# A post-norm decoder layer on one core: one visit per unit for attention's weighted values, two turns of duties, and six low parts on GpSimd

## What is computed

```python
x = layernorm(x + attention(x, w_qkv, w_o))        # 32 heads of 32, 8 key/value heads, RoPE, causal
x = layernorm(x + cross(x, ctx, Wq, bq, Wk, bk))   # softmax((xWq'+bq)(cWk'+bk)'/32) c
x = layernorm(x + ffn(x))                          # x @ W' + bias, W looked up from 4-bit codes
```

## Time and profile before

| | |
|---|---|
| runs, median (lowest to highest) | 1291.42 us (1290.22 to 1291.81) |
| the profiled execution, its own time | 1288.92 us |
| its span, first to last instruction | 1287.1 us |
| TensorE matmuls busy | 1263.6 us, 98% |
| VectorE busy | 901.6 us, 70% |
| ScalarE busy | 531.4 us, 41% |
| GpSimd busy | 477.2 us, 37% |
| granted TensorE clock, mean | 0.999 of full |

### The profile page before, as it was taken

One profiled execution on the slowest core, in us unless ns is written; L12 is line 12 of the kernel. 1 busy time (PEld: TensorE's weight loads), 2 busy tenths in 40 slices (PEclk: granted clock), 3 DMA queues, 4 the chain that ended last, 5 costly groups with the idle time before them and its releaser, 6 DMA issues.

```text
span 1287.1 us, 25356 instructions
## 1 busy us (share of the span) xinstructions
PE 1263.6 (98%) x8230; PEld 1041.7 (81%) x8230; DVE 901.6 (70%) x2526; ACT 531.4 (41%) x1597; POOL 477.2 (37%) x413
## 2 busy tenths in 40 slices
PE   8999999998999999999999999999999999999997
PEld 6887888997777777777777887888888888888886
DVE  7999898578888888888876974353443636556665
ACT  4131212457777777777760223243433433100110
POOL 3512122345656656656550000544334450222221
PEclk9999999999999999999999999999999999999999
DMA  7165435463864344344343215125251419212221
GB/s 280 68 213 170 144 132 203 141 208 113 236 182 120 118 134 127 114 135 134 121 127 106 68 34 173 41 82 181 66 196 64 149 49 358 100 65 98 98 87 60
DMA packets 135450, 170.43 MB, mean 132 GB/s; under 512 B 36688, under 2 KB 100176, under 8 KB 134736
## 3 DMA queue, kind: packets, MB, share of 16 engines
q1 hardware_dynamic: 135376, 169.47, 40.6%
HBM read 112.80 MB, written 56.62 MB: 132 GB/s over the span
## 4 chain that ended last, share of the span: by engine, by line
PE 72%; issue 12%; DVE 8%; POOL 4%; SPq 2%; DMA 1%; ACT 1%; POOLq 0%; DVEq 0%; ACTq 0%
PE bank L863 13%; PE bank L677 11%; PE bank L679 11%; PE bank L678 11%; PE bank L805 7%; PE bank L763 4%; PE bank L790 4%; POOL x2b L1984 3%; PE bank L834 3%; PE bank L838 2%; PE bank L726 1%; DVE bits L1482 1%; PE bank L982 1%; DVE pick_b L1521 1%; DVE pick_c L1510 1%
## 5 line engine op out<-in xcount | busy, mean ns | idle before, releaser
L1907 POOL TENSOR_TENSOR prob<-prob,rinv 128x512 f32<-128x512 f32 x192 | 205.5, 1071 | 204.8 <-DVE rinv L1570 204.7
L1187 ACT ACTIVATE prob<-bank,nmax 128x256 f32<-128x256 f32 (+1 forms) x512 | 211.3, 427 | 90.6 <-DVE nmax L1562 83.9
L1562 DVE CUSTOM_DVE_ANT_0 bank<-bank,mask 128x256 f32<-128x256 f32 (+1 forms) x512 | 169.3, 383 | 7.3 <-PE bank L790 3.7
L805 PE MATMUL bank<-ident,prob 128*128 128x128 f32 x768 | 122.0, 282 | 2.8 <-ACT probT L1117 2.8
L805 PEld LDWEIGHTS bank<-ident,prob 128*128 128x128 f32 x768 | 85.4, 141 | 35.9 <-issue 16.7
L1187 ACT ACTIVATION_READ_ACCUMULATOR prob<-bank,nmax 128x1 f32 x512 | 108.1, 211 | 0.0
L1723 DVE SCALAR_TENSOR_TENSOR k_lo<-bank,bA,k_hi 128x512 fp32r<-128x512 f32 x32 | 24.0, 751 | 115.1 <-ACT k_hi L1320 114.5
L790 PE MATMUL bank<-k,q 96*128 96x256 f32 (+1 forms) x512 | 102.8, 303 | 1.7 <-DMA vv<-v_scr 1.7
L863 PE MATMUL bank<-wo_hi,att_hi 128*128 128x512 f32 x256 | 103.9, 406 | 0.0
L677 PE MATMUL bank<-f_hi,x2T_hi 128*128 128x512 f32 x256 | 101.0, 395 | 0.8 <-DVE x2T_lo L1418 0.8
L677 PE MATMUL bank<-cT_hi,m_hi 128*128 128x512 f32 x256 | 100.4, 392 | 0.7 <-DVE cT_lo L1418 0.7
(11 more groups left out here) (201 smaller groups left out, 3145.9 us busy)
## 6 DMA issues: line engine op xcount, KB each, us to landing
q<-qk_scr SPq DMA_DIRECT2D x192, 128.0 KB, 2.4
x_st<-x_scr SPq DMA_DIRECT2D x32, 512.0 KB, 3.8
qk_scr<-rot SPq DMA_DIRECT2D x60, 256.0 KB, 2.6
xc_in<-x_cols SPq DMA_DIRECT2D x32, 256.0 KB, 4.7
y<-x SPq DMA_DIRECT2D x16, 512.0 KB, 3.6
x_scr<-y SPq DMA_DIRECT2D x16, 512.0 KB, 2.7
cx_in<-ctx_in SPq DMA_DIRECT2D x16, 512.0 KB, 4.9
x_scr<-x_st SPq DMA_DIRECT2D x16, 512.0 KB, 3.3
```

What stands on the lines that cost most here:

```text
L805: mm = nc.tensor.transpose(tb[:, at * P:(at + 1) * P], prob[:, k % 4, c:c + P], ident[:, :])
L1187: mm = nc.scalar.activation(prob[:, k % 4, i * keys:(i + 1) * keys], SBANK[pos][:, i * keys:(i + 1) * keys], ACT.Exp, bias=nmax[:, k % 4, ...
L1562: mm = nc.vector.tensor_tensor_reduce(part, part, mask[:, 2 * P - keys:2 * P], 1.0, BIGGEST, ALU.add, ALU.min, nmax[:, k % 4, i:i + 1])
L1907: nc.gpsimd.tensor_tensor(pr, pr, rinv[:, k % 4, 0:n].unsqueeze(2).to_broadcast([P, n, keys]), ALU.mult)\
```

## The change

Four edits.

1. `weighted` does nothing at positions 0 and 1. At position 2 it waits for all three copies of the transposes and does both halves: two groups of four, `pv_done`, one group of four, `pv_done`.
2. A turn of a decoded block is made inside the pair that follows, behind its second slice (`TURN_KT`, 12 matmuls in), instead of ahead of it.
3. VectorE's order where x's low parts and decoding steps alternate is given by a table (`X_LOW_AFTER`): in group 0 all eight low parts first; in groups 1 and 2 two decoding steps stand ahead of the first low part.
4. The six low parts of w_o that are made in the first batch go from VectorE to GpSimd, with a semaphore of their own for the other two; block 5's step moves from 22 to 21, the last two blocks' and the last RoPE item's steps of batch 1 move by one.

```diff
+        X_LOW_AFTER = ((0,) * KT, (2, 2, 3, 3, 4, 4, 5, 5), (2, 2, 3, 3, 4, 5, 5, 6))
+        TURN_KT = 2
-        WO_STEPS = {(0, 12): 2, (0, 14): 3, (0, 18): 0, (0, 19): 1, (0, 20): 4, (0, 22): 5, (1, 4): 6, (1, 6): 7}
+        WO_STEPS = {(0, 12): 2, (0, 14): 3, (0, 18): 0, (0, 19): 1, (0, 20): 4, (0, 21): 5, (1, 5): 6, (1, 7): 7}
...
                 for kt in range(KT):
+                    if turned is not None and kt == TURN_KT:
+                        turn_f(turned)
...
-                pos, unit = k % 3, k // 3
-                if pos == 0:
+                unit = k // 3
+                if k % 3 < 2:
                     return
-                taken(b, k - 1)
-                taken(b, k)
+                for i in range(3):
+                    taken(b, k - 2 + i)
...
-                if pos == 1:
-                    wait(pe, att_ready, KVH * b + unit)
-                    for t in range(2):
-                        for h in range(REP):
-                            src = probT[:, (k - 1 + h // 2) % 4, (2 * t + h % 2) * P:(2 * t + h % 2 + 1) * P]
...
-                else:
+                wait(pe, att_ready, KVH * b + unit)
+                for t in range(2):
                     for h in range(REP):
-                        mm = nc.tensor.matmul(OBANK[HD * h:HD * (h + 1), 0:P], v[:, 0, :],
-                                              probT[:, k % 4, h * P:(h + 1) * P], start=True, stop=True,
-                                              skip_group_check=True)
+                        src = probT[:, (k - 2 + h // 2) % 4, (2 * t + h % 2) * P:(2 * t + h % 2 + 1) * P]
+                        mm = nc.tensor.matmul(OBANK[HD * h:HD * (h + 1), P:2 * P], v[:, t, :], src,
+                                              start=t == 0, stop=t == 1, skip_group_check=True)
+                mm.then_inc(pv_done, 1)
+                for h in range(REP):
+                    mm = nc.tensor.matmul(OBANK[HD * h:HD * (h + 1), 0:P], v[:, 0, :],
+                                          probT[:, k % 4, h * P:(h + 1) * P], start=True, stop=True,
+                                          skip_group_check=True)
                 mm.then_inc(pv_done, 1)
...
-                    if age == 1 and k == 2:
+                    if age == 1 and k == 3:
                         rope_item(11)
...
-                    if age < 2 and (age, k - 1) in WO_STEPS:
+                    if age == 1 and (age, k - 1) in WO_STEPS:
                         kt = WO_STEPS[age, k - 1]
                         dve.wait_ge(wo_hi_ready, WO_TURN[kt] + 1)
-                        low(wo_lo[:, kt, :], wo_in[:, kt, :], wo_hi[:, kt, :]).then_inc(wo_lo_ready, 1)
+                        low(wo_lo[:, kt, :], wo_in[:, kt, :], wo_hi[:, kt, :]).then_inc(wo_lo2_ready, 1)
...
+                    if age == 0 and (0, k - 1) in WO_STEPS:
+                        kt = WO_STEPS[0, k - 1]
+                        pool.wait_ge(wo_hi_ready, WO_TURN[kt] + 1)
+                        nc.gpsimd.tensor_tensor(wo_lo[:, kt, :], wo_in[:, kt, :], wo_hi[:, kt, :].bitcast(F32), ALU.subtract)\
+                            .then_inc(wo_lo_ready, 1)
```

More of the change, by code:

```diff
@@ L243, in decoder_layer @@
         fps_ready, f_hi_ready, f_lo_ready, f_stored = sem("fps_ready"), sem("f_hi_ready"), sem("f_lo_ready"), sem("f_stored")
-        wo_ld, wo_hi_ready, wo_lo_ready = sems("wo_ld", KT // 2), sem("wo_hi_ready"), sem("wo_lo_ready")
+        wo_ld, wo_hi_ready, wo_lo_ready, wo_lo2_ready = (
+            sems("wo_ld", KT // 2), sem("wo_hi_ready"), sem("wo_lo_ready"), sem("wo_lo2_ready"))
         wq_first_ld, wq_ld, wq_hi_ready, wq_lo_ready = sem("wq_first_ld"), sem("wq_ld"), sem("wq_hi_ready"), sem("wq_lo_ready")
@@ L330, in decoder_layer @@
         LOW_STEP = {23: (0, 0), 0: (1, 1), 2: (1, 2), 6: (1, 3)}
-        WO_STEPS = {(0, 12): 2, (0, 14): 3, (0, 18): 0, (0, 19): 1, (0, 20): 4, (0, 22): 5, (1, 4): 6, (1, 6): 7}
+        WO_STEPS = {(0, 12): 2, (0, 14): 3, (0, 18): 0, (0, 19): 1, (0, 20): 4, (0, 21): 5, (1, 5): 6, (1, 7): 7}
+        WO_EARLY = sum(age == 0 for age, _ in WO_STEPS)
         WO_TURN = {kt: i for i, kt in enumerate(WO_STEPS.values())}
@@ L694, in turn_f, with qk_pair @@
                 turn(decode_tiles(b)[1][:, :].bitcast(F32), banks, fps_ready)
-            def qk_pair(g, c):
+            def qk_pair(g, c, turned=None):
                 n = PAIRS * g + c
@@ L730, in values @@
                         mm.then_inc(x_lo_used if low else x_used, 1)
-            for at in ORDER:
+            for i, at in enumerate(ORDER):
                 if at[1] < PAIRS:
-                    qk_pair(*at)
+                    qk_pair(*at, F_TURN.get(ORDER[i - 1]) if i else None)
                 else:
@@ L738, in _ @@
                     pe.wait_ge(consts_step, 4)
-                if at in F_TURN:
-                    turn_f(F_TURN[at])
             def fill(k):
@@ L818, in weighted @@
             def weighted(b, k):
-                pos, unit = k % 3, k // 3
-                if pos == 0:
+                unit = k // 3
+                if k % 3 < 2:
                     return
-                taken(b, k - 1)
-                taken(b, k)
+                for i in range(3):
+                    taken(b, k - 2 + i)
                 v = vv[unit % SLOTS]
-                if isinstance(b, int) and b == 0 and k == 1:
+                if isinstance(b, int) and b == 0 and unit == 0:
                     pe.wait_ge(f_lo_ready, 2 * EARLY)
-                if pos == 1:
-                    wait(pe, att_ready, KVH * b + unit)
-                    for t in range(2):
-                        for h in range(REP):
-                            src = probT[:, (k - 1 + h // 2) % 4, (2 * t + h % 2) * P:(2 * t + h % 2 + 1) * P]
-                            mm = nc.tensor.matmul(OBANK[HD * h:HD * (h + 1), P:2 * P], v[:, t, :], src,
-                                                  start=t == 0, stop=t == 1, skip_group_check=True)
-                else:
-                    for h in range(REP):
-                        mm = nc.tensor.matmul(OBANK[HD * h:HD * (h + 1), 0:P], v[:, 0, :],
-                                              probT[:, k % 4, h * P:(h + 1) * P], start=True, stop=True,
-                                              skip_group_check=True)
+                wait(pe, att_ready, KVH * b + unit)
+                for t in range(2):
+                    for h in range(REP):
+                        src = probT[:, (k - 2 + h // 2) % 4, (2 * t + h % 2) * P:(2 * t + h % 2 + 1) * P]
[6 more added lines that the diff above has]
+                                          skip_group_check=True)
                 mm.then_inc(pv_done, 1)
@@ L859, in project @@
                     if g == 0 and ps == 0:
-                        pe.wait_ge(wo_lo_ready, WO_TURN[kt] + 1)
+                        if WO_TURN[kt] < WO_EARLY:
+                            pe.wait_ge(wo_lo_ready, WO_TURN[kt] + 1)
+                        else:
+                            pe.wait_ge(wo_lo2_ready, WO_TURN[kt] - WO_EARLY + 1)
                     lt = att_lo if ps == 2 else att_hi
@@ L1229, in stage2_batch @@
                         rope_high(item_pair((k - 3) // 2))
-                    if age == 1 and k == 3:
+                    if age == 1 and k == 4:
                         rope_high(item_pair(11))
@@ L1546, in _ @@
                     f_low(F_TURN[g, c])
[L1547 to L1551, removed]
+                steps = EARLY_STEPS[STEP_END[g, c] - STEPS_OF[g, c]:STEP_END[g, c]]
+                marks = [0] + list(X_LOW_AFTER[g]) if c == PAIRS - 1 else [0]
+                for i, at in enumerate(marks):
+                    if i:
+                        x_low(g + 1, i - 1)
+                    for go in steps[at:marks[i + 1] if i + 1 < len(marks) else len(steps)]:
                         go()
```

## The result

The changed kernel takes **1283.81 us** (median of 5 runs, 1283.10 to 1285.21) where the kernel before takes 1291.42 on the same chip: ratio 0.9941, 95% interval 0.9929 to 0.9952. That is faster by 7.6 us; 20.6 were forecast, and 1283.8 lies above the range, which ended at 1277. The two profiled executions are 5.1 us apart (spans 1287.1 and 1282.0). What follows counts between them.

What follows compares the result with a forecast made beforehand. TensorE's own order of work was taken to bound the kernel. Gains of 17.6 + 1.4 + 1.6 + 0 = 20.6 us from 1291.42 gave 1270.8 us, range 1266.4 to 1277.

Steps and rivals of the forecast that it cites:

- What bounds the kernel: Whole kernel: TensorE's own order of work sets the time; its matmuls fill 98% of the span, 50.00 of 50 us in the loop.
- The cost of a visit: TensorE's 32-wide matmuls: 0.31 us fixed per visit, 0.21 per group of four; merging saves 0.31 per unit, 17.6 us in all.
- Rival B: Merged visits: the fixed 0.31 us belongs to each operand group, so edit 1 gains nothing; 1288.8 us, chance 0.06.
- The new wait for three copies asks for nothing later than the old one did. These cost nothing.: Merged visit at position 2: its wait and what is queued behind the moved matmuls were counted at no cost.
- Rival C: Loop: VectorE sets the pace, 41.25 us of work in 47.5; half of 46 units' saving becomes waits, 1278 us, chance 0.09.
- an unevenness of a microsecond is covered by the three steps between scores and transposes: Loop: the argument against VectorE setting the pace; its uneven work would not hold TensorE up. No size of its own.
- Rival D: Position 0 in the loop: transposes come 1.04 us sooner and wait for scaled probabilities; 1294 us, slower than before, chance 0.03.
- Edits 2 and 3: Stage one: moved turns remove a 1.4 us wait; reordered low parts of x remove three waits, 1.6 us.
- The transposes cost the same in either place: Turns of decoded blocks: the eight transposes cost no more inside the next pair, leaving edit 2 its 1.4 us gain.
- Edit 4: w_o's six low parts on GpSimd: 0 us, one delay replacing another at the change of batch; between 1.3 gain and 6 loss.
- rival A: GpSimd late: w_o parts stretched by 1.86 beside VectorE delay RoPE item 10 and unit 2's scores by 6 us; 1277, chance 0.14.
- The tail: End of the last batch: the first visit's two groups now stand behind the second's wait for a copy, costing 0.4 us.

Runs made afterwards that it cites:

- copy-first run: The changed kernel with ScalarE's copy of the third position's turned probabilities ahead of the third position's exponent, from batch 1 on; 1274.65 us, ratio 0.9880.
- both exchanges: The changed kernel with that copy ahead of the third exponent and the two normalisations of x1 one step later; 1274.03 us, ratio 0.9880.

## Why the prediction was wrong

*What bounds the kernel* was right for the kernel before, and it hid the failure: 50.00 us busy of 50 says that TensorE never waited, not by how much the others were ahead of it.

*The cost of a visit* was right. 0.33 and 0.79 us were measured for 0.33 and 0.78, 0.29 us per unit in batch 0 for 0.31, 5.96 us per undisturbed unit for 5.94. Rival B falls.

*"The new wait for three copies asks for nothing later than the old one did. These cost nothing."* **This is the step that failed.** The first sentence is true, the second does not follow. The copy of position 2 had been met with 0.06 us to spare at the place shown. In a loop that is sped up as a whole, every wait is met earlier; what matters is whether the thing waited for comes earlier too. This one did not: its ring (visit, turn, VectorE's copies, maxima, exponent, copy) has most of its length on VectorE and ScalarE, 452.91 to 470.48 in the stretch shown, where nothing was saved. Where it passes through a visit it even grew, by 0.43 us (0.79 against 0.36), as the 16 records moved in from the step before. Instead of 46 x 0.31 = 14.3 us, the loop gave 7.77 - 5.44 = 2.3.

*Rival C* (1278) had half of the mechanism. VectorE's work does hold the visits up, but by where it stands: 0.81 us of it one step later took most of the longest stop away. The rival looked at VectorE's total, 41.25 us of 50, and dismissed its bursts because "an unevenness of a microsecond is covered by the three steps between scores and transposes". Those steps cover the path from the scores to the transposes. The copy behind the transposes has its cover elsewhere, in ScalarE's order, and there it was nil. That VectorE's total is no bound is shown by the copy-first run, where its load rose to 42.52. *Rival D* looked at position 0, whose transposes never waited in the loop.

*Edits 2 and 3* together: 3.15 us for 3.0. The split was wrong: 0.4 and 2.75 where I had 1.4 and 1.6. "The transposes cost the same in either place" overlooked another turn, the one between groups 0 and 1, which covered a wait for VectorE. Edit 3 then removed that wait. That the sum came out is in part luck: edit 2 gave 1.0 us less than forecast, and edit 3 more than its own upper bound of 2.4. The size of edit 3 was taken from the list of waits, three of 1.6 us together. From start to start they cost more: the changed kernel is 0.68 us ahead at the first scores (210.97 before) and 3.15 at those of position 2 (219.68 before), 2.47 us over the same three stops.

*Edit 4* was right at 0, and rival A falls: each of the six w_o parts on GpSimd took 2.37 to 2.40 us, unstretched, and the store of item 10 began at 309.67, 7.85 us ahead of unit 2's scores (7.93 before). Two rows of GpSimd and one of VectorE:

```profile
304.45 2.37 POOL L1932 TENSOR_TENSOR wo_lo<-wo_in,wo_hi 128x1024 fp32r<-128x1024 f32 x1
306.79 1.48 POOL L1914 TENSOR_TENSOR prob<-prob,rinv 128x512 f32<-128x512 f32 x1
...
305.15 2.22 DVE L1424 TENSOR_TENSOR att_lo<-att,att_hi 128x512 fp32r<-128x512 f32 x1 [0.34 <-ACT att_hi L1123]
```

The two engines did clash, but it was VectorE that paid. The w_o part began first and took its usual time. VectorE's subtraction of att_lo, begun inside it at 305.15, took 2.22 us where 0.67 to 0.69 is usual, and ended 0.55 us behind it. The changed kernel's trace has 15 subtractions of att_lo that began inside an operation of GpSimd, and each ended 0.55 us behind that operation's end. The other way round, the scaling at 306.79, begun inside VectorE's subtraction, took 1.48 us for 1.04. So whichever began second paid, with what was left of the first, and not in the proportion of 1.86 that rival A used. The Trainium skill (GPSIMD Engine Reference, Key points) says that GpSimd contends with VectorE's instructions of two SBUF inputs; the trace agrees.

*The tail*, -0.4 us forecast, cost 1.1. It is the same ring, which runs out there:

```profile
655.75 0.63 PE L809 MATMUL bank<-ident,prob 128*128 128x128 f32 x4 [1.18 <-ACT probT L1123]
...
659.72 0.54 PE L837 MATMUL bank<-probT,vv 128*32 128x128 f32 x12 [0.98 <-ACT probT L1123]
```

With the copy first the wait of 1.18 us is not there; the second is still 0.89 us (651.24), and one of 0.57 us for GpSimd's scaling stands ahead of it (647.35). Of the 15.6 us that that kernel is ahead at (7, 23), 15.2 reach the end. The 0.4 lost is the size of the forecast's term, though made up of other waits.

**What is left between the copy-first kernel and the forecast.** Its ratio of 0.9880 to 1291.42 is 1275.9 us, 5.1 above 1270.8. Its ledger reads 2.9 (stage 1), 1.7 (batch 0), 0.6 (batch 1), 10.3 (six loop batches), -0.4. Against eight units by 0.31 us, 2.48 a batch, it lacks 4.6 us in the loop, of which the two remaining stops are 6 x 0.58 = 3.5, and 1.8 in batch 1, where the loads' queue holds; the forecast had counted two of batch 1's units as lost, and two of the last batch's. The rest of the loop, 0.2 us a batch, is in pieces too small to name.

## What to carry to other kernels

Before a saving on the busiest engine is counted, ask of every wait in that loop how late it was met, not only whether it shows as a wait: the end of the producer beside the start of the consumer gives it in two rows. Where several engines work in fixed orders, follow each wait back until the path closes on itself; only work inside such a ring, or a shorter ring, makes it turn faster. An operation that is ready should not stand behind one that waits for another engine: here exchanging the two was worth some 8 us (0.9880 of before against 0.9941), and nothing before the change had made them critical.

## What the runs showed of the hardware

Single DMA issues on SP's queue, usually 0.42 to 0.45 us, now and then take 0.7 to 2.1. They are at other places in each trace of batch 1:

```profile
311.51 2.09 SPq L462 DMA_DIRECT2D q<-qk_scr  x1
313.64 0.43 SPq L465 DMA_DIRECT2D k<-qk_scr  x1
```

These rows are of the run with both exchanges. In the three runs where an issue of 1.88 to 2.09 us falls between 311 and 315 us, the scores of unit 2 wait 2.56 to 2.81 us; in the changed kernel, with one of 1.32 us, they wait 0.99. The other runs with that load in its old place have long issues of 1.11 to 1.65 us and waits of 0.87 to 2.35, in no common order (1.94 us of wait with an issue of 1.11, 1.33 with one of 1.54). The cause was not sought.

TensorE's granted clock fell twice in the changed kernel, for some 3 us. It was 0.52 (the lower level, 1.2 GHz) behind the 16 matmuls with two rows and the 16 that give two columns (738.63 to 741.46), with matmuls 0.43 us apart; before, the same work at 742 to 749 kept 1.00. Windows of the changed kernel (busy PE, PEld, DVE, ACT, POOL, then the granted clock):

```profile
739.00:742.00 3.00, 3.00 (x34) 2.90 (x34) 2.60 (x7) 0.60 (x2) 0.00 (x0) 0.99 0.61 180
742.00:745.50 3.50, 3.50 (x10) 2.73 (x9) 3.50 (x21) 1.06 (x1) 0.00 (x0) 0.52 0.03 5
```

Another fall followed the wait of 1.76 us at the change of batch (308 to 311 us: 0.58). Eight spacings of 0.43 for 0.23 are the ledger's 1.6 us. It is no part of what the change does: other kernels here with the same merged visit kept 1.00 in that stretch, and without it the two profiled executions would be 6.7 us apart, nearer to the 7.6 of the medians. That is no proof: another execution of the changed kernel had a mean granted clock of 1.000 and took 1283.80 us, the same as the profiled one with 0.996. The other fall lies ahead of a wait for a load. What decides whether an execution gets them was not settled.
